# DLRM tower with a two-layer CIN: a unit's work and the weight sums in another order

## The reference, cut to what matters

```python
e = stack([tbl_f[ids[:, f]] for f in range(32)], axis=1)          # 1024, 32, 32
x1 = einsum('bpd,pj->bjd', outer(e, e), W0)                        # 1024 pairs -> 128
x2 = einsum('bpd,pj->bjd', outer(e, x1), W1)                       # 4096 pairs -> 128
z = concatenate([x1, x2], axis=1).sum(axis=-1)                     # 1024, 256
h = relu(concatenate([z, dense_ctx], axis=1) @ W_top1 + b_top1)
h = relu(h @ W_top2 + b_top2)
y = h @ W_top3
```

## Time and profile before

| what | value |
|---|---|
| median of 3 runs | 376.28 us (376.24 to 376.7) |
| the profiled execution | 377.52 us |
| its span, first to last instruction | 375.7 us |
| busy: PE, ACT, POOL, DVE | 86%, 62%, 67%, 54% of the span |
| mean granted clock of TensorE | 0.982 of 2.4 GHz |

### The profile page before, as it was taken

The page is one execution under the profiler, slowest core; times in us unless marked ns, Lnnn a source line. Parts: engine busy times, 40 slices in busy tenths (PEclk is TensorE's granted clock), DMA queues, the critical chain, the costliest instruction groups (busy, mean ns, idle before and its releaser), DMA issues.

```text
span 375.7 us, 11560 instructions
## 1 busy us (share of the span) xinstructions
PE 323.7 (86%) x4680; PEld 298.8 (80%) x4680; DVE 203.2 (54%) x834; ACT 233.9 (62%) x774; POOL 252.3 (67%) x262
## 2 busy tenths in 40 slices
PE   1899936249998999899989998998699879989897
PEld 1677735248998999899989988988698878889797
DVE  4336999933665565555646663655455544554201
ACT  1578566187667766776686667666676557556601
POOL 5777887877777777777777777777777777740000
PEclk9999996699999999999999999999999999999999
DMA  7801001010100010000101000100010001100000
GB/s 220 312 14 16 11 9 16 9 16 14 16 16 16 14 16 16 16 16 15 16 13 17 15 17 15 15 15 15 15 16 14 16 15 17 15 10 2 3 2 0
DMA packets 10773, 9.79 MB, mean 26 GB/s; under 512 B 4664, under 2 KB 8896, under 8 KB 10720
## 3 DMA queue, kind: packets, MB, share of 16 engines
q0 software_dynamic: 8192, 4.21, 7.5%
q1 hardware_dynamic: 2528, 4.84, 3.8%
HBM read 9.03 MB, written 0.00 MB: 24 GB/s over the span
## 4 chain that ended last, share of the span: by engine, by line
POOL 66%; issue 21%; PE 10%; DMA 1%; ACT 1%; POOLq 0%; DVE 0%; SPq 0%
POOL emb L278 66%; PE WA L726 4%; PE M L739 1%; PE PA L687 1%; DMA emb<-in_table,rows 1%; PE QB L698 1%; DMA base<-in_bases 1%; PE M L758 1%; PE M L749 0%; POOLq L81 0%; ACT h L358 0%; PE T L711 0%; PE T L787 0%; PE M L750 0%; PE ET L787 0%
## 5 line engine op out<-in xcount | busy, mean ns | idle before, releaser
L278 POOL DMA_INDIRECT emb<-in_table,rows x256 | 251.6, 983 | 80.4 <-issue 77.8
L726 PE MATMUL WA<-TS,RX 128*128 128x128 f32 x896 | 111.0, 277 | 1.0 <-ACT TS L285 1.0
L726 PEld LDWEIGHTS WA<-TS,RX 128*128 128x128 f32 x896 | 104.6, 192 | 4.1 <-issue 4.0
L584 DVE COPY TS<-T 32x64 f32<-32x64 f32 x256 | 55.5, 217 | 76.7 <-PE T L711 69.7
L285 ACT ACTIVATE eblk<-ET 32x256 f32<-32x256 f32 x128 | 48.7, 380 | 55.3 <-PE ET L674 53.0
L687 PE MATMUL PA<-eblk,zP 128*128 128x132 f32 x512 | 75.0, 282 | 1.9 <-ACT TS L285 1.1
L552 DVE TENSOR_TENSOR zQ<-ET,eT 128x1024 f32<-128x1024 f32 x32 | 39.2, 1225 | 65.2 <-ACT eT L285 65.1
L285 ACT ACTIVATE TS<-T 32x64 f32<-32x64 f32 (+1 forms) x320 | 66.5, 208 | 7.7
L687 PEld LDWEIGHTS PA<-eblk,zP 128*128 128x128 f32 x512 | 66.7, 195 | 2.7 <-ACT TS L285 1.3
L546 DVE TENSOR_TENSOR zP<-ET,eT 128x224 f32<-128x224 f32 (+6 forms) x224 | 47.7, 289 | 0.0
L285 ACT ACTIVATE TS<-PA 128x396 f32<-128x396 f32 (+1 forms) x96 | 44.5, 463 | 2.7 <-PE PA L687 1.6
(11 more groups left out here) (87 smaller groups left out, 290.5 us busy)
## 6 DMA issues: line engine op xcount, KB each, us to landing
emb<-in_table,rows POOLq DMA_INDIRECT x256, 2.4
TS<-in_W SPq DMA_DIRECT2D x8, 256.0 KB, 5.6
wt<-in_W_top SPq DMA_DIRECT2D x2, 512.0 KB, 8.3
y1w<-in_W_rows SPq DMA_DIRECT2D x1, 448.0 KB, 6.7
TS<-in_W_rows SPq DMA_DIRECT2D x1, 448.0 KB, 7.3
sym<-in_W_cols SPq DMA_DIRECT2D x1, 264.0 KB, 3.0
TS<-in_W_cols SPq DMA_DIRECT2D x1, 264.0 KB, 3.3
idc<-in_ids SPq DMA_DIRECT2D x1, 128.0 KB, 2.1
```

The lines of the kernel that those rows point to most:

```text
L278: eng.indirect_dma_start(emb[par][:, g, :], None, table, bass.IndirectOffsetOnAxis(rows[:, k, g:g + 1], 0))\
L584: eng.tensor_copy(view(ts[32 * q:32 * q + 32, :, :], P * REST + b0, [[4 * P, 2], [P, 4], [1, 8]]), view(src, q, [[C17, 2], [4, 4], [C33, 8 ...
L726: m = eng.matmul(WA[:, 0:P], C[:, kt, :], TS[k % 2][:, slot_of(kt), :], start=(kt == 0), stop=(kt == KT - 1))
```

## The change

- **A unit's order on TensorE:** first what else there is to do (`fill(u)`), then two trios, `across_triples`, `other_triples`, the third trio; `emb_transposes(u + 1)` comes last, behind them, and not ahead of unit `u`'s trios. Three units are transposed while the weights are multiplied (steps 10, 20, 31), before it was two (8, 18).
- **ScalarE** copies `ET` to `eT` first (`e_copy`) and spreads `eT`, not `ET`, into `eblk`; in the weight steps one of the four copies per step.
- **VectorE:** the pairs inside a part of 8 fields are ordered as blocks of 4x4, 2x2, 2x2 and 4 singles (`BLOCKS`), so that `products` has 8 instructions and not 11, and the sums fewer and larger ones. `products` waits only for `eT`, and the first trio only for the first five products.
- **Weight sums and transposes:** the sums run in the order in which the transposes use them, with a semaphore for each class; `weights(n)` go into units 3 to 6 (four, four, four and two calls) and are copied back in place (`C` is gone). `second(0)` runs between them, in the order `KT_ORDER`.
- **Top network spread:** `second(k)` in shares of 9, 13, 19 and 15 blocks over the next tile's units; `first` behind the last of them, `hidden1` at that unit's end, `hidden2` and `result` in the two units after. Tile 6's blocks are done by unit 30, its `hidden1` goes to unit 31's start, its `hidden2` behind unit 31, its `result` inside `last_tile`.

```diff
@@ -24,9 +24,13 @@
...
+def part_pairs():
+
+
+    pairs = [(a, 4 + b) for a in range(4) for b in range(4)]
+    pairs += [(4 * n + a, 4 * n + 2 + b) for n in range(2) for a in range(2) for b in range(2)]
+    pairs += [(2 * j, 2 * j + 1) for j in range(4)]
+    return pairs
...
+    NZ = 8
+    BLOCKS = ((0, 0, 4), (HALF, 0, 2), (HALF + 4, 4, 2), (HALF + SUB, 0, 1))
...
@@ -211,31 +220,60 @@
...
+        KT_ORDER = [*range(HALF, F), *range(HALF), *range(F, KT)]
...
+        FIRST_UNIT = ((), (), (), (0, 1, 2, 3), (4, 5, 6, 7), (8, 9, 10, 11), (12, 13), ())
...
+        def pieces(k):
+
+            if k == 0:
+                return (0, 16, 28, 44, KT)
+            if k == END - 1:
+                return (0, 18, 38, KT, KT)
+            return (0, 9, 22, 41, KT)
...
+        EARLY_AT = (10, 20, F - 1)
+
+        def ahead(u):
+
+            if u == 1:
+                return 3
+            return u + 1 if 3 <= u < ALL - 1 else None
...
@@ -292,18 +330,22 @@
...
+            def e_copy(u):
+
+                eng.wait_ge(et_made, u + 1)
+                copy(eT[:, :], ET[:, 0:GROUPS * F]).then_inc(eT_made, 1)
+
+            def eblk_copy(u, v):
+
+                if u == 0 and v == 0:
                     eng.wait_ge(zeroed, 5)
                     eng.wait_ge(ones_set, 4 * NQ)
-                eng.wait_ge(et_made, u + 1)
-                wait(eng, t3_made, u - 1)
-                for v in range(NQ):
-                    r = slice(DIM * v, DIM * v + DIM)
-                    dst = view(eblk[u % 2][r, :, :, :], 2 * C17 * v + 1, [[EB, GROUPS], [C17, 2], [1, HALF]])
-                    copy(dst, ET[r, 0:GROUPS * F].rearrange("p (g x h) -> p g x h", x=2, h=HALF)).then_inc(eblk_made, 1)
-                copy(eT[:, :], ET[:, 0:GROUPS * F]).then_inc(eblk_made, 1)
+                if v == 0:
+                    eng.wait_ge(eT_made, u + 1)
+                    wait(eng, t3_made, u - 1)
+                r = slice(DIM * v, DIM * v + DIM)
+                dst = view(eblk[u % 2][r, :, :, :], 2 * C17 * v + 1, [[EB, GROUPS], [C17, 2], [1, HALF]])
+                copy(dst, eT[r, :].rearrange("p (g x h) -> p g x h", x=2, h=HALF)).then_inc(eblk_made, 1)
...
@@ -376,36 +417,53 @@
...
+                for i, at in enumerate(EARLY_AT):
+                    if h == at:
+                        e_copy(i)
+                    if at < h <= at + NQ:
+                        eblk_copy(i, h - at - 1)
...
+            for u in range(ALL):
+                k, i = divmod(u, UNITS)
+                mine = list(FIRST_UNIT[u]) if u < len(FIRST_UNIT) else []
+                others = list(range(by_vector(u - 1), NQ)) if u > 0 else []
+                if u == 1:
+                    for v in range(NQ):
+                        eblk_copy(2, v)
+                if u == 2:
+                    e_copy(3)
+                if u >= len(EARLY_AT):
+                    if u > 3:
+                        e_copy(u)
+                    if k >= 2 and i == 0:
+                        hidden1(k - 2)
+                    if 0 < len(mine) < 5:
+                        c_copy(mine.pop(0))
+                    for v in range(NQ):
+                        eblk_copy(u, v)
+                while mine or others:
+                    if mine:
+                        c_copy(mine.pop(0))
+                    if others:
+                        rest_copies(u - 1, others.pop(0))
+                if u == ALL - 1:
+                    hidden1(END - 1)
+                if k >= 2 and i == 1:
+                    y_copy(k - 2)
+                if k >= 1 and i == (2 if k == END else 3):
+                    y2_copy(k - 1)
+                    y1_copy(k - 1)
+                part_copy(TRIOS * u)
+                part_copy(TRIOS * u + 1)
+                across_copy(u)
+                part_copy(TRIOS * u + 2)
+                if k >= 2 and i == 0:
+                    hidden2(k - 2)
+            hidden2(END - 1)
+            for j in range(by_vector(ALL - 1), NQ):
                 rest_copies(ALL - 1, j)
+            y_copy(END - 1)
             y1_copy(END)
...
@@ -429,27 +487,57 @@
...
+            def steps(w, by_first, by_second):
+
+
+                if w == 1:
+                    return [[2 * (by_first + by_second), 4]]
+                return [[by_first, w], [by_second, w]]
+
+            def pairs_at(w):
+                return [[1, 4]] if w == 1 else [[w, w], [1, w]]
...
+                to_c, to_other = (1, HALF) if X == 0 else (HALF, 1)
+                row, col = HALF * (1 - X) + c0, 32 * (2 * X + e)
+                for at, f, w in BLOCKS:
+                    dst = rt(row, col + at, [[RTC, cn]] + pairs_at(w))
+                    h, other = (f + w, f) if second else (f, f + w)
+                    by = (to_other, RAB) if second else (RAB, to_other)
+                    add(dst, dst, rx_at(X, SUB * e + h, c0, SUB * e + other, [[to_c, cn]] + steps(w, *by)), s_done)
+                if not second:
+                    dst = rt(row, col + PAIRS, [[RTC, cn], [1, 4]])
+                    add(dst, dst, rx_at(X, SUB * e, c0, SUB * e, [[to_c, cn], [RAB + to_other, 4]]), s_done)
...
@@ -504,31 +597,39 @@
...
+            def high_sums():
+
+                eng.wait_ge(rt_kept, F)
+                eng.wait_ge(rx_kept, F // 2)
+                own_firsts(1)
+                both_across(0, SUB, SUB, False, high_first)
+                own_seconds(1)
+                eng.wait_ge(high_first, 8)
+                both_across(0, SUB, SUB, True, high_added)
...
+            def low_sums():
+
+                apart_across(1, 1, 0, HALF, False, low_first)
+                cross_first(0, SUB, SUB, cross_made)
+                eng.wait_ge(low_first, 5)
+                apart_across(1, 1, 0, HALF, True, low_added)
...
@@ -541,50 +642,50 @@
...
+                if part == 0:
+                    eng.wait_ge(eT_made, u + 1)
+                    wait(eng, t3_made, u - 1)
+                    wait(eng, p_made, TRIOS * (u - 1))
...
+                    some = [[SUB, parts], [1, 4]]
+                    eng.tensor_tensor(view(within, PAIRS, [[32, parts], [1, 4]]), field(0, some), copied(0, some),
                                       ALU.mult).then_inc(z_made, 1)
-
-                if part == 0:
-                    eng.wait_ge(eblk_made, (NQ + 1) * (u + 1))
-                    wait(eng, t3_made, u - 1)
+                if part == 1:
                     eng.tensor_tensor(view(across, 0, [[64, sides], [SUB, SUB], [1, SUB]]),
                                       field(0, [[HALF, sides], [1, SUB], [0, SUB]]),
                                       copied(SUB, [[HALF, sides], [0, SUB], [1, SUB]]), ALU.mult).then_inc(z_made, 1)
...
+            def all_products(u):
+                for part in range(3):
+                    products(u, part)
...
@@ -603,23 +704,32 @@
...
+            all_products(0)
             eng.wait_ge(rt_kept, HALF)
-            own_sums(0)
+            own_firsts(0)
+            own_seconds(0)
+            all_products(1)
             early_sums()
-            for u in range(ALL):
-                if u > 0:
-                    for part in range(3):
-                        rest_copies(u - 1, part)
-                if len(EARLY_AT) <= u + 1 < ALL:
-                    for part in range(3):
-                        products(u + 1, part)
-                if u < 3:
-                    late_sums(u)
-            for part in range(3):
-                rest_copies(ALL - 1, part)
+            high_sums()
+            rest_copies(0, 0)
+            rest_copies(0, 1)
+            all_products(2)
+            rest_copies(1, 0)
+            rest_copies(1, 1)
+            all_products(3)
+            rest_copies(2, 0)
+            rest_copies(2, 1)
+            low_sums()
+            for u in range(UNITS, ALL):
+                rest_copies(u - 1, 0)
+                all_products(u)
+                rest_copies(u - 1, 1)
+                if u == UNITS:
+                    cross_sums()
+                if u == UNITS + 1:
+                    rest_sums()
+            for j in range(by_vector(ALL - 1)):
+                rest_copies(ALL - 1, j)
...
@@ -645,24 +755,21 @@
...
+            def weights(n):
+
+                if n == 0:
+                    eng.wait_ge(high_added, 2 * 7)
+                    eng.wait_ge(own_added[1], 2 * 4)
+                elif n == 4:
+                    eng.wait_ge(low_added, 2 * 4)
+                    eng.wait_ge(own_added[0], 2 * 4)
+                elif n == 8:
+                    eng.wait_ge(cross_added, 3)
+                elif n == 12:
+                    eng.wait_ge(rest_added, 6)
+                wait(eng, c_kept, n - 1 if n <= 4 else n)
                 for x in range(4):
-                    kt = 4 * q + x
-                    if kt < F:
-                        piece = RT[:, kt, 0:P]
-                    elif kt < F + HALF:
-                        piece = QC[:, kt - F, :]
-                    else:
-                        n = 4 * (kt - F - HALF)
```

(93 more changed lines are left out.)

267 lines of the change are left out of this document (102 added, 165 removed).

## The result

The changed kernel takes 375.13 us in the median of 20 runs (371.39 to 377.37), the kernel before, beside it on the same chips, 376.7 (20 runs, from 375.98). The ratio is 0.9939 (95% interval 0.992 to 0.9959): 0.6% faster, not the 2.4% forecast, and above the range of 364 to 371. The profiled execution took 371.39 us, the fastest of the 20; its span is 369.6. Ratios are taken over fast executions alone (those within 1.5% of their kernel's fastest), so a ratio is not always the quotient of the two medians beside it.

The account below looks back on a forecast made before the run. The end was set by the last gather's landing, unchanged at 334.90, plus TensorE's remaining work, 40.8 us cut to 31.35 + 0.3: span 366.6, median 367.1 us; forecast 365 to 369, range 364.0 to 371.0.

Parts of the forecast that it names:

- the gathers: Gather issue on GpSimd beside VectorE's sums: 9.4 us loss unchanged, at most 1.5 us worse; last landing stays at 334.9.
- Rival B: Weight sums on VectorE: merged, longer adds hold the gathers up more, giving 368.5 to 370.5 us; chance 0.08.
- Rival E: Whole kernel: nothing changes, only if the last gather came some 9 us later; chance 0.02.
- C: Early weight sums spare the gathers: loss falls by a third, median 364, or by half, 362.5; chance 0.06.
- A: Units 27 to 30 have no slack and come late on TensorE: 369.5 to 374.5 us; chance 0.13.
- D: Chain from transposes to products stays uncovered in each unit: slower above 1.3 us exposed, 402 with all 2.4; chance 0.05.
- the signs of being wrong: Last landing moves over 2 us, transposes of units 28–31 no longer await gathers, or middle-unit trios wait for `eblk` or `z`.
- The tail: TensorE's work after the last gather lands: 40.8 us becomes 31.35 + 0.3, a gain of 9.15 us.
- a tile takes 35.2 us of TensorE: TensorE's work per tile: falls from 36.2 to 34.8 us, mostly because the wait of `hidden2` for ScalarE goes.
- Unit 8: Early part: TensorE reaches unit 8's transposes at about 115 us; several us of error would not matter, hidden by gathers.
- The waits for gathers: TensorE's waits for gathered rows: grow from 9.5 to over 20 us and start near unit 16.
- The four copies from `eT`: ScalarE's spreading of `eT` into `eblk`: between half and twice 1.59 us, taken as 1.59.

Follow-up runs that it names:

- before_no_short: Kernel before without its shortest weight-sum adds (diagonals at distance 6 and 7 of the sums over `RX`), so some sums are missing: 383.66 us, ratio 1.0178.
- after_split32: Changed kernel with the 84 adds of the triangle and squares cut into 180 pieces of at most 32 elements: 375.72 us, ratio 0.9924.
- after_ahead: Changed kernel with the next unit's transposes put back ahead of the trios from unit 4 on: 381.23 us, ratio 1.0121.
- after_drain: Changed kernel with VectorE waiting for each add's own result, behind 90 of the 94 adds: 362.48 us, ratio 0.9614.
- before_pause: Kernel before with a one-column memset behind each of its 130 two-input adds: 369.55 us, ratio 0.9799.
- after_pause: Changed kernel with a one-column memset behind each of VectorE's 94 two-input adds: 365.11 us, ratio 0.9681.

## Why the prediction was wrong

**The step that failed** is the gathers: "I take 0", bounded by a loss of "a sixth", 1.5 us, and so "Last landing as before, 334.9". The loss grew by 3.6 us in the fastest execution (last landing 336.0 + 2.4 = 338.4), some 7 in the median (loss near 17, the estimate above). The sum erred in what it took for the harm: "the long adds, of 512 and 1024 elements, stay as they are and do most of the harm", and 36 fewer small adds at best spare something. The small adds were a way out for the gathers (before_no_short: fewer adds, 15.4 - 9.4 = 6.0 us more of loss). The bound was wrong because a hold was priced by the add that the gather meets. A hold can last for most of the run of adds that it lies in. The row behind this step was misread, too: the gather of 2.32 us began at 69.06 and the sum of 1.88 us only at 70.57; most of the time between went to seven adds of 112 elements and fewer:

```profile
69.33 1.33 DVE L421 TENSOR_TENSOR RT<-RT,RX 128x112 f32<-128x112 f32 x7
```

Whether the longer holds come from the merging or from the new order of the sums is not shown. No run makes the old adds in the new order, and after_split32, which undoes much of the merging in pieces of 32, kept its loss at 16.7.

The Trainium skill, page "SBUF — State Buffer", section "Summary: rules for kernel authors", says that of a VectorE instruction with two SBUF inputs and a GpSimd instruction that reads SBUF the second to issue is blocked until the first finishes. The trace agrees on who blocks whom (memsets, which read nothing: no loss), but not on for how long: one gather outlasted more than twenty adds in a row (7.69 us, 12.12 in before_no_short), and no single add here takes over 2 us.

**Rival B** had the sign and the place right (chance 0.08) and stopped at 370.5. **Rival E** said that nothing would be left if the last gather came some 9 us later, "which nothing but a doubling of the loss would do"; the median's loss near 17 is not far from that doubling. C has the wrong sign for this change, but its mechanism is real: with the loss at 2.3 the kernel takes 362.48. A and D did not happen: TensorE's one wait for a product is the 2.0 us for `zQ` in the list above, none is for `eblk`. Of the signs of being wrong that the prediction named, two came: the last landing moved by 3.5 us, and no transposes of units 28 to 31 wait for a gather (the last wait is unit 27's), though unit 31's start 0.2 us behind the landing.

**What was right.** The tail: 31.35 + 0.3 forecast from the landing, 31.0 measured from the transposes, which start 0.2 after it. `second` of the last tile starts 8.9 us behind the transposes (9.05 forecast), the third trio waits 0.61 for the bank. From 118.06 to 153.28 a tile takes 35.2 us of TensorE (34.8 forecast); `hidden2` waits no more, but `result` now does, 4.6 us in five waits (the row of L878 above). after_ahead gives 3.8 us of the gain back by the order alone. Unit 8 was reached at 118.06, 3 us later than forecast, and as forecast it did not matter: the first wait for a gather after the held one comes at 178.67, unit 15.

```profile
118.06 0.38 PE L781 MATMUL ET<-ident,emb 128*128 128x128 f32 x2
...
153.28 0.38 PE L781 MATMUL ET<-ident,emb 128*128 128x128 f32 x2
...
178.67 0.44 PE L781 MATMUL ET<-ident,emb 128*128 128x128 f32 x2 [1.36 <-DMA emb<-in_table,rows]
```

The waits for gathers grew to 15.7 us, not over 20. The four copies from `eT`, bounded by half and twice 1.59 us, took 1.75 from 339.53 on, near the 1.59 that was taken.

So the change is worth 9.6 us behind the last gather, by its order and its spread top network, and gave back 3.6 to some 7 by its weight sums, and what the sums do to the gathers was taken as 0.

## What to carry to other kernels

Where GpSimd issues gathers at a pace that sets the end, look at what VectorE runs beside them: a run of two-input adds without a break can stop the issue for most of its length (up to 12.12 us here). Making such adds fewer and larger, or putting them in another order, need not be a saving; a wait of VectorE for its own result, behind every add or every third, brought this kernel from 0.994 to 0.961 and 0.963 of the time before. And when two edits come together, price them apart, by the resource that each one touches.

## What was not expected of the hardware

A gather of 0.94 us stood up to 12.12 us, and the same kernel ran between 371.39 and 377.37 us; that its holds make this spread is argued from the runs with stops (1.0 us in after_drain), not shown, since one execution was profiled. Still open is what frees a gather without a stop: in the kernel before, adds of 16 and 32 elements did; in after_split32, pieces of 32 did not between 38 and 44 us, and from 45.30 a gather passed such pieces in 0.95 us; a memset of one column did in before_pause (1.60 us at most), in after_pause at some adds and at others not (3.44 us). In the changed kernel only the stop freed every gather within a few adds, and what in the stop does it was not measured by itself.
